# Context rows of two cross attentions loaded in 1 KB pieces, and probabilities transposed in contiguous blocks

## What is computed

```
x = x + xattn0(layernorm(x), ctx, mask, ...)        # layer 0
...
x = x + xattn1(layernorm(x), ctx, ...)              # layer 1

def xattn(query, ctx, ...):
    Q = query @ Wq + bq;  K = ctx @ Wk + bk;  V = ctx @ Wv + bv
    energy = Q @ K.T / 16                            # 64 x 1601 a batch
    (layer 0: rows with mask 0 are set to -1e10)
    out = softmax(energy) @ V                        # layer 0: then @ Wfc + bfc
```

## Time and profile before

| what | value |
|---|---|
| median of 3 runs | 978.25 us |
| the profiled execution: span | 991.7 us |
| TensorE busy | 760.3 us, 77% |
| VectorE, ScalarE, GpSimd busy | 468.2, 261.5, 269.1 us |
| DMA traffic | 200.37 MB in 70779 packets, mean 202 GB/s |
| queue of SP (q1) | 60720 packets, 176.29 MB |
| first attention, roughly | 5 to 161 us |
| second attention, roughly | 288 to 431 us |
| columns, a tile | 3202 KB, one DMA, 8 in each attention |
| rows, a tile | 3072 KB + 130 KB, two DMAs, 8 of each in each attention |
| `w_wf` | 2048 KB, one DMA, 8.3 us from issue to landing |

### The profile page before, as it was taken

How to read it: one execution, slowest core, us unless ns; L and a number is a source line. 1 busy time by engine, 2 the same in 40 slices (tenths; PEclk the granted TensorE clock), 3 DMA queues, 4 the chain that set the end, 5 groups by cost and what they waited for, 6 DMA issues and landing times. The chain is left out here.

```text
span 991.7 us, 19372 instructions
## 1 busy us (share of the span) xinstructions
PE 760.3 (77%) x6571; PEld 498.9 (50%) x6571; DVE 468.2 (47%) x1284; ACT 261.5 (26%) x519; POOL 269.1 (27%) x304
## 2 busy tenths in 40 slices
PE   6699999776869989889988897447756766657647
PEld 4365566455535555564457775225544544433215
DVE  4423245775745323235638858885523322322226
ACT  1211224644502121222733302231111211111150
POOL 1020002012412000000415612314555555554420
PEclk9899998986859999979985569877878799786878
DMA  9999982000896999712963001016566666668867
GB/s 344 387 341 413 404 361 82 5 2 26 305 323 260 345 411 390 318 33 60 209 154 88 16 3 43 1 49 183 178 187 195 199 197 190 187 175 251 248 222 297
DMA packets 70779, 200.37 MB, mean 202 GB/s; under 512 B 11912, under 2 KB 37744, under 8 KB 64944
## 3 DMA queue, kind: packets, MB, share of 16 engines
q1 hardware_dynamic: 60720, 176.29, 51.6%
q0 software_dynamic: 7680, 20.98, 6.9%
q10 hardware_dynamic: 2304, 2.10, 0.7%
HBM read 185.51 MB, written 13.83 MB: 201 GB/s over the span
## 5 line engine op out<-in xcount | busy, mean ns | idle before, releaser
L1996 PE MATMUL ps<-moe_wgu,moe_xgT 128*128 128x256 f32 (+1 forms) x320 | 108.7, 472 | 82.8 <-issue 47.3
L1996 PEld LDWEIGHTS ps<-moe_wgu,moe_xgT 128*128 128x128 f32 (+1 forms) x320 | 62.9, 220 | 106.1 <-issue 79.1
L2118 POOL DMA_INDIRECT moe_xg<-xn_rows,moe_idx x80 | 78.4, 980 | 126.7 <-DVE moe_idx L2067 76.7
L2127 POOL DMA_INDIRECT y_rows<-moe_ysb,moe_row x80 | 79.4, 992 | 38.7 <-issue 24.6
L2080 DVE TENSOR_TENSOR moe_hrow<-moe_hs,ps 128x128 f32<-128x128 f32 x80 | 23.0, 287 | 141.2 <-ACT moe_hs L2102 95.3
L2102 ACT ACTIVATE moe_hs<-ps 128x128 f32<-128x128 f32 x80 | 22.3, 279 | 193.4 <-PE ps L1996 100.5
L1469 POOL TENSOR_TENSOR ss_dec<-ss_dec,ss_cT 128x256 f32<-128x256 f32 x48 | 39.9, 865 | 92.7 <-ACT ss_dec L1424 51.1
L2013 PE MATMUL ps<-moe_wdn,moe_hT 128*128 128x256 f32 (+1 forms) x160 | 59.0, 458 | 0.1
L1282 PE MATMUL ps<-xnT,w_win 128*128 128x512 f32 x128 | 58.5, 616 | 0.0
L2075 DVE COPY moe_xgT<-ps 128x256 f32<-128x256 f32 x80 | 33.9, 424 | 45.2 <-remote 18.8
L1314 PE MATMUL ps<-ss_dec 64*64 64x32 f32 (+2 forms) x1792 | 46.2, 255 | 11.1 <-issue 9.6
(11 more groups left out here) (404 smaller groups left out, 1436.6 us busy)
## 6 DMA issues: line engine op xcount, KB each, us to landing
x0ctxT<-ctx_T SPq DMA_DIRECT2D x8, 3202.0 KB, 19.4
x1ctxT<-ctx_T SPq DMA_DIRECT2D x8, 3202.0 KB, 13.8
x0ctxN<-ctx SPq DMA_DIRECT2D x8, 3072.0 KB
x1ctxN<-ctx SPq DMA_DIRECT2D x8, 3072.0 KB
moe_wgu<-moe_gate_up SPq DMA_DIRECT2D x80, 256.0 KB
moe_wdn<-L_ffn_We_down SPq DMA_DIRECT2D x80, 128.0 KB
moe_yg<-y_rows SPq DMA_DIRECT2D x7, 1024.0 KB, 11.0
ss_dec<-seg_rows SPq DMA_DIRECT2D x8, 768.0 KB, 17.2
```

Of the source, the lines that this page charges most:

```text
L1996: mm = pe.matmul(ps[c * n_:(c + 1) * n_, 2 + a2, 0:2 * FE], xgT[:, a2, h, c * n_:(c + 1) * n_], src[:, a4, h, :, :].rearrange("p x f -> p ...
L2118: nc.gpsimd.indirect_dma_start(out=xg[:, a4, :], out_offset=None, in_=xn_rows, in_offset=bass.IndirectOffsetOnAxis(ap=idx[:, a4:a4 + 1], a ...
L2127: nc.gpsimd.indirect_dma_start(out=y_rows, out_offset=bass.IndirectOffsetOnAxis(ap=row[:, a4:a4 + 1], axis=0), in_=ysb[:, a4, :], in_offse ...
```

## The change

`load_rows` brings the 12 x 128 positions with one DMA for each of the two batches instead of one for both, and puts position 128c + k into chunk c of partition k: 12 pieces of 256 floats (1 KB) for each partition, 128 rows apart in DRAM. The transposes of `prob` then read 128 contiguous columns for each chunk. The 65 positions left over are loaded as before. The rows' semaphore now rises by 48 a tile instead of 32.

```diff
         def load_rows(eng, q, u, ctxN, s):
-            eng.dma_start(ctxN[:, u, :, 0:KC, :].rearrange("p b c d -> p b (c d)"),
-                          a["ctx_1024"][ds(q * 2, 2), 0:KC * P, :].rearrange("b (p c) d -> p b (c d)", c=KC)
-                          ).then_inc(s[u], 16)
+            for b in range(2):
+                eng.dma_start(ctxN[:, u, b, 0:KC, :],
+                              a["ctx_1024"][ds(q * 2 + b, 1), 0:KC * P, :].rearrange("o (c p) d -> p (o c) d", p=P)
+                              ).then_inc(s[u], 16)
             eng.dma_start(ctxN[0:KR, u, :, KC, :],
                           a["ctx_1024"][ds(q * 2, 2), KC * P:NK, :].rearrange("b p d -> p b d")).then_inc(s[u], 16)
...
-            rr = x_done[0] * 32 * (NT // 2)
+            rr = x_done[0] * 48 * (NT // 2)
...
                             k = P if c < KC else KR
-                            src = prob[:, u, c:KC * P:KC] if c < KC else prob[:, u, KC * P:NK]
+                            src = prob[:, u, c * P:c * P + k]
...
-                    pe.wait_ge(s_ctx[u], q * 32 + rr + 32)
+                    pe.wait_ge(s_ctx[u], q * 48 + rr + 48)
```

## The result

| | time, us |
|---|---|
| changed kernel | median 1017.23 (1006.27 to 1018.61, 4 runs) |
| kernel before, beside it | median 979.25 (977.93 to 981.25, 4 runs) |
| ratio | 1.0332 [1.026, 1.0405] |
| the profiled execution after | 1018.61, its span 1016.8 (before: span 991.7) |

The change makes the kernel slower by 3.3%, some 32 us (25 to 40 by the interval). That is the direction forecast and twice the size: 15.6 us were predicted, and the time lies outside the range.

A forecast was written before the change was run, and what follows sets the result against it. Late tiles of both attentions were taken to be bound by DMA transfers. Dearer row loads +15.0, transposes -1.1 and clock +1.7 gave +15.6 us, from the 978.25 us median to 993.8 us; range 983 to 1006.

The forecast's parts named there:

- At nothing: One more issue on SP a load, 0.4 us, taken as hidden by the full queue; 6 us the limit if empty.
- The last line of the prediction: Signs of being wrong: rows over 410 GB/s, PVs over 19 us apart, or delay from SP standing in its issues.
- First attention: At tile 6's probabilities-by-context product (PV): seven dearer row loads delay it, 7 x 1.25 = +8.75 us.
- The price of a load: A tile's main row load in 1 KB pieces at the FFN weights' 365 GB/s: 8.62 instead of 7.37 us, +1.25.
- Second attention: At tile 6's probabilities-by-context product (PV): five dearer row loads delay it, 5 x 1.25 = +6.25 us.
- Transposes: Contiguous reads save TensorE 0.38 us a tile, counted at three places where no wait follows: -1.1 us.
- The clock: TensorE idles more, so tile 6's PV may run at a lower clock: +1.7 us, counted once for both attentions.
- Rival 1: Packets cost nothing, rows keep 427 GB/s, only the transposes' gain is left: 977.2 us, no difference; chance 0.12.
- rival 3: TensorE is the bound after all and the transposes' full 6.1 us count: 972.1 us; chance 0.04.
- rival 2: Row pieces cost as much as the ACT queue's stores, 54 ns each, 12 x 3.0 = 36 us: 1015 us; chance 0.12.

The follow-up runs named there:

- experiment 2: Changed kernel with the rows of tile 1 of the second attention issued in the attention's own block, behind the FFN's barrier: 1000.76 us, ratio 1.0173.
- 10: Changed kernel with tile 1's rows behind the FFN's block, tile 4's columns before the latent weights, mixer's weights after the last rows: 999.44 us, ratio 1.0142.
- experiment 3: Kernel before with contiguous transposes alone, loads as before, so probabilities and context rows no longer match: 983.35 us, ratio 0.9973.

## Why the prediction was right in direction and half the size

**The step that failed** is the paragraph "At nothing", which put the issues on SP at no cost. It gave SyncE's issue 0.4 us, "hidden since the queue holds several us of work whenever SP issues rows". The full queue is what makes the issue long: with 96 pieces an engine in each of two DMAs, SyncE stood in the issues of one tile's rows for 9.52 + 5.02 us. I counted what that issue delays on SyncE's own queue and never asked who waits for SyncE. At tile 1 of the second attention it is every engine, in the meeting that ends the FFN's block. That costs 10.2 us in the profiles and 11 when it is taken away (experiment 2). The last line of the prediction named such a delay as what would make it wrong, and the earlier trace rows had one to learn from: 8.21 us in a single issue. I used the number and did not ask what it would be with more pieces.

**First attention, forecast +8.75, found +11.8.** The same stalls in the issues are the first part. The SyncE timeline after, answering to the earlier trace rows:

```profile
55.53 8.31 SPq L203 DMA_DIRECT2D x0ctxN<-ctx  x2
63.88 5.09 SPq L206 DMA_DIRECT2D x0ctxN<-ctx  x1
...
78.66 0.40 SPq L199 DMA_DIRECT2D x0ctxT<-ctx_T  x1
```

Tile 4's columns leave at 78.66, 6.9 us later than before, where 75.5 was forecast. SyncE gets past the rows of tile 2 only at 68.97 and then issues 16 small loads one after another, while the queue runs dry: from 72 to 79 us it moved 0.68 MB where it had moved 2.26 before. That these 3.1 us beyond the forecast come from the stall is read from the timeline; no run took it away alone. From there to PV of tile 6 it is 4.9 us more than before, the part that I had put at 5.0 for four dearer loads.

**The price of a load, forecast +1.25 us, found +1.67.** 3.146/0.348 = 9.04 against 7.37 us. The FFN weights were the right kind of row and an optimistic one. The dearer price did not show in full. Over four loads it makes 6.7 us instead of 5.0, but from tile 4's columns to PV of tile 6 the two attentions grew by 4.9 and 5.1 us. A step of the second attention grew by 1.42 us (16.49 to 17.91 on the mean of three), not 1.67; why a step did not grow by the whole price stays open.

**Second attention, forecast +6.25, found +6.3.** Partly luck. The parts fit: tile 4's columns leave 1.2 us later after the first scores (48.42 instead of 47.21 us, forecast 1.25), and the way to PV of tile 6 is 5.1 us longer (forecast 5.0). But the measured price of a load would give 5 x 1.67 = 8.4 us. So the right total stands on a price that was too low and on steps that grew by less than the price.

**Transposes, forecast -1.1, found less.** The weight loads fell to 141 ns as forecast, but eight transposes in a row went from 1.28 to 1.09 us and the last five then wait 0.24 us for ScalarE's copy. A tile saves 0.13 to 0.18 us, not 0.38, and the two steps from PV of tile 6 to PV of tile 7 are 0.2 us shorter each. In sixteen tiles that is at most 16 x 0.18 = 2.9 us, if nothing hid it.

**The clock, forecast +1.7, not seen at the place named.** PV took 7.46, 7.20, 7.85 and 8.66 us after idling 4.55, 2.88, 5.59 and 3.39 us, but PV of tile 6, the one that counts, took 5.83 in both attentions. The term exists all the same: in experiments 2 and 10 it hit PV of tile 6 of the first attention (7.50 and 7.52 us), and the step to tile 7 took 11.3 us instead of 9.7.

**The rivals.** Rival 1 (packets free) and rival 3 (TensorE bound) fell with the 348 GB/s and with experiment 3. My price was 45 ns a piece (8.62 us by 192), rival 2's 54, the measured one 47. Rival 2's total of 1015 us is close to the result, but for another reason: its mechanism would have put PVs over 19 us apart, and they are 17.6 and 17.9.

By terms, with what the runs showed: 11.8 - 0.2 + 10.2 + 6.3 = 28.1 us at the end of the second attention; forecast 15.6. Of the difference of 12.5, the barrier is 10.2, and the first attention 3.1.

## What to carry to other kernels

A load in many small pieces cost twice here: on the DMA engines for each piece, and on the engine that issued it, which stood in the issue while the queue still held earlier pieces. So ask of every issue what the issuing engine has to reach next, and above all whether all engines meet there. Before paying for a faster read on the compute side, see whether late tiles wait because of the order in the queue: moving the mixer's weights behind the loop was worth 5.6 us (1.7 to 9.6), where all the transposes together could have given 2.9. And when a load is moved, look at what now stands behind it: the 16 small loads let the queue run low ahead of tile 4's columns and behind them alike.

## What the runs showed of the hardware that I had not expected

- The time of SyncE in one issue isn't a constant. In the first attention it was a median of 0.34 us with 12 KB pieces (up to 2.4), 0.62 with 4 KB (up to 3.5) and 2.99 with 1 KB (up to 11.1), for the same bytes. With the queue just run dry, two 1 KB issues together took 1.28 us.
- A piece costs 9.5 ns of a DMA engine beside 37.6 ns a KB, an estimate from two of the three sizes; 1, 4 and 12 KB pieces of these rows ran at 348, 410 and 427 to 433 GB/s, with a busy share over 1 in all of them.
- A transpose's weight load that reads every fourth fp32 takes 213 ns, every twelfth 223, and contiguous 141. In the chain of a tile that was worth only 0.13 to 0.18 us for 12 transposes.
- Executions of one and the same kernel differ by 10 us in the mixture of experts alone (270 and 280 us), nearly as much as the largest single effect found here.
